# Transposes of attention and experts moved from TensorE to transposing DMAs, in a vision transformer block with routed experts

## The reference

```python
p = x.reshape(n, C, 14, 16, 14, 16).transpose(0, 2, 4, 1, 3, 5).reshape(n, 196, 768)
h = concat([class_token, einsum('npd,hd->nph', p, W) + b], 1) + pos_embed     # 64 x 197 x 192
# local attention: 12 heads of 16, each token sees the 13 tokens around it
q, k, v = split(layernorm(h) @ w_qkv)
h = h + (softmax(q . k_window / 4) . v_window) @ w_proj + b_proj
# experts: 8, the best 2 of each token, weights made to sum to 1
probs = softmax(layernorm(h) @ router_w.T)
top_w, top_i = top_k(probs, 2)
h = h + sum_e w_e * (gelu(layernorm(h) @ w1[e] + b1[e]) @ w2[e] + b2[e])      # 192 -> 768 -> 192
```

## Time and profile before

| | us |
|---|---|
| median of 3 runs | 1631.99 (1623.08 to 1639.81) |
| profiled execution | 1638.75 |
| its span, first to last instruction | 1637.0 |
| busy: TensorE, VectorE, GpSimd, ScalarE | 1471.8, 1114.5, 856.6, 721.7 |
| mean granted TensorE clock | 0.959 of full |

### The profile page before, as it was taken

One profiled execution on the slowest core, in us unless ns is written; L12 is line 12 of the kernel. 1 busy time (PEld: TensorE's weight loads), 2 busy tenths in 40 slices (PEclk: granted clock), 3 DMA queues, 4 the chain that ended last, 5 costly groups with the idle time before them and its releaser, 6 DMA issues. The chain is left out here.

```text
span 1637.0 us, 52314 instructions
## 1 busy us (share of the span) xinstructions
PE 1471.8 (90%) x18345; PEld 1222.1 (75%) x18346; DVE 1114.5 (68%) x2883; ACT 721.7 (44%) x1209; POOL 856.6 (52%) x900
## 2 busy tenths in 40 slices
PE   5999999998989999998643999999999999999995
PEld 4787888877878887887532777777777777777774
DVE  2577878777877787776554666666666666666663
ACT  2455554454545544454222444444444444444441
POOL 4235665555655665565441555555555555555554
PEclk9999999999999999999656999999999999999998
DMA  5665656556565657554314344444344444444432
GB/s 168 176 180 157 195 142 189 158 158 190 148 189 145 198 141 200 153 149 114 91 43 142 59 60 59 61 61 64 59 59 59 61 59 61 59 61 61 65 36 30
DMA packets 190165, 182.64 MB, mean 112 GB/s; under 512 B 86362, under 2 KB 166438, under 8 KB 188990
## 3 DMA queue, kind: packets, MB, share of 16 engines
q1 hardware_dynamic: 125834, 111.46, 25.1%
q0 software_dynamic: 41680, 41.84, 17.4%
q10 hardware_dynamic: 22499, 27.28, 5.3%
HBM read 104.93 MB, written 65.29 MB: 104 GB/s over the span
## 5 line engine op out<-in xcount | busy, mean ns | idle before, releaser
L992 POOL DMA_INDIRECT out<-y,token x219 | 368.6, 1683 | 73.6 <-issue 72.8
L1100 PE MATMUL down<-w_hi,g_hi 128*128 x1314 | 323.6, 246 | 2.1 <-DVE y L1066 1.1
L1102 PE MATMUL down<-w_hi,g_lo 128*128 x1314 | 323.0, 246 | 0.0
L1101 PE MATMUL down<-w_lo,g_hi 128*128 x1314 | 322.9, 246 | 0.0
L1088 PE MATMUL up<-e_xT,w_hi 128*128 128x384 f16 x1314 | 286.7, 327 | 0.0
L1013 ACT ACTIVATE act_out<-up,bias 128x384 f32<-128x384 f32 x438 | 251.2, 582 | 73.1 <-PE up L1088 73.0
L390 POOL DMA_INDIRECT sorted_scratch<-payload,place x212 | 220.1, 1038 | 59.7 <-issue 56.7
L779 PE MATMUL near<-we,patches 128*120 128x192 f32 x1272 | 223.9, 333 | 18.6 <-DMA patches<-in_xt 10.9
L1005 ACT COPY e_xT<-turned 128x1152 f16<-128x1152 f16 x73 | 81.7, 1119 | 353.0 <-PE turned L1080 353.0
L779 PEld LDWEIGHTS near<-we,patches 128*120 128x120 f32 x1272 | 208.1, 185 | 28.9 <-issue 28.1
L1049 DVE TENSOR_TENSOR g_lo<-act_out,g_hi 128x768 f16<-128x768 f32 x219 | 210.0, 959 | 7.6
(11 more groups left out here) (155 smaller groups left out, 2680.9 us busy)
## 6 DMA issues: line engine op xcount, KB each, us to landing
patches<-in_xt SPq DMA_DIRECT2D x53, 720.0 KB
rows<-sorted_scratch SPq DMA_DIRECT2D x73, 301.5 KB, 2.8
v_diag<-v_scratch SPq DMA_DIRECT2D x159, 89.2 KB
v_scratch<-v_rows SPq DMA_DIRECT2D x53, 191.2 KB, 3.3
tab<-tab_scratch SPq DMA_DIRECT2D x53, 180.0 KB
out<-h ACTq DMA_DIRECT2D x52, 180.0 KB
stage<-in_w ACTq DMA_DIRECT2D x8, 1152.0 KB
k_diag<-qk SPq DMA_DIRECT2D x424, 15.8 KB
```

The source lines that it names most:

```text
L992: pool.indirect_dma_start(out=out, out_offset=bass.IndirectOffsetOnAxis(ap=token[k][:, n:n + 1], axis=0), in_=y[k % 2][:, n, :], in_offset ...
L1100: pe.matmul(dst, g_hi[k % 2][:, m, cols], high, start=(m == 0), stop=False)
L1101: pe.matmul(dst, g_hi[k % 2][:, m, cols], low, start=False, stop=False)
L1102: ins = pe.matmul(dst, g_lo[k % 2][:, m, cols], high, start=False, stop=(m == MF - 1))
```

## The change

Seven sets of edits:

- `turn` and the identity are gone. SP issues a transposing DMA (`transpose=True`, SBUF to SBUF) for the normalised tokens, one for the attention output, and two for the routed tokens. `xs1` and `payload` get 128 partitions, and are cleared at the start; TensorE waits for the DMAs' semaphores `x1_in` and `x2_in`. ScalarE's copies 480 and 491 are gone; copy 485 now reads the transposed slots in SBUF, and waits for `oT_in`.
- TensorE's order: the probabilities' transposes stand ahead of counting.
- VectorE: `route_steps(grp, 2)` stands behind the normalisation, together with part 3.
- SP's order: transpose of the normalised tokens, 8 key copies, transpose of the output, transposes of the routed tokens, `v_diag`. The key copies and `v_diag` stand one iteration earlier in SP's stream.
- Value store, patches (now two blocks ahead), table and mask are issued by ScalarE, behind the high halves of the normalised tokens.
- The tables are built in `v_diag` and no longer in `payload`, so that `v_diag` is cleared after they are stored.
- Experts: each batch is loaded transposed straight from the sorted DRAM scratch into one of four `e_xT` buffers, and its 18 last columns (number, weights) by a second DMA. The transposes, `take` and the PSUM tensor `turned` are gone; four up banks in place of three.

```diff
@@ SP, attention_part
             def body(t):
-                g, a = t - 2, t - 4
-                if runs(t, 4):
+                g, a, d, b = t - 1, t - 3, t - 5, t - 6
+                if runs(t, 1):
+
+                    sp.wait_ge(s["lo1"], g + 1)
+                    need(sp, s["v_done"], g)
+                    sp.dma_start(xT1[:].rearrange("p n c r -> p (n c) r"), xs1[:].rearrange("p n c -> p (n c)"), transpose=True)\
+                      .then_inc(s["x1_in"], 16)
+                if runs(t, 3):
 
                     sp.wait_ge(s["qk_lo_set"], min(a + 2, BLOCKS))
                     need(sp, s["scored"], 2 * a)
                     for h in range(8):
                         sp.dma_start(*key_halves(h, a)).then_inc(s["k_diag_set"], 16)
+                if runs(t, 5):
+
+                    sp.wait_ge(s["o_lo_set"], d + 1)
+                    need(sp, s["oT_set"], d)
+                    sp.dma_start(oT_slots[:].rearrange("p n c r -> p (n c) r"), os_[:].rearrange("p n c -> p (n c)"), transpose=True)\
+                      .then_inc(s["oT_in"], 16)
+                if runs(t, 6):
+
+                    sp.wait_ge(s["lo2"], b + 1)
+                    need(sp, s["routed"], b)
+                    for n in range(2):
+                        sp.dma_start(xT2[:, n], payload[:, 2 * (b % RING) + n, 0:NUMBER_AT].bitcast(F16), transpose=True)\
+                          .then_inc(s["x2_in"], 16)
...
@@ ScalarE, attention_part
                 if runs(t, 5):
 
-                    act.wait_ge(s["o_turned"], d + 1)
+                    act.wait_ge(s["oT_in"], 16 * (d + 1))
                     need(act, s["proj_done"], d)
...
+                if runs(t, 1):
+
+                    act.wait_ge(s["v_set"], g + 1)
+                    act.dma_start(v_dram[REACH + SPAN * g:REACH + SPAN * g + SPAN, :].rearrange("(n p) c -> p n c", n=2),
+                                  v_rows[:].rearrange("p n h d -> p n (h d)")).then_inc(s["v_out"], 16)
+                if runs(t + 2, 0):
+                    act.wait_ge(s["embedded"], t + 1)
+                    act.dma_start(patches[t % 2][:], xt[t + 2]).then_inc(s_patch[t % 2], 16)
+                    if t == 0:
+                        act.wait_ge(s["tab_out"], 16)
+                    act.wait_ge(s["h1_set"], t + 1)
+                    load_tab(act, t + 2)
+                if runs(t, 3) and a + 1 < BLOCKS:
+                    need(act, s["scored"], 2 * a)
+                    load_band(act, a + 1)
...
@@ TensorE, attention_part
                 if runs(t, 1):
 
-                    pe.wait_ge(s["xT_set"], g + 1)
+                    pe.wait_ge(s["x1_in"], 16 * (g + 1))
                     need(pe, s["qk_main"], g)
...
                 if runs(t, 6):
 
-                    pe.wait_ge(s["xT2_set"], b + 1)
...
+                    pe.wait_ge(s["x2_in"], 32 * (b + 1))
+                    pe.wait_ge(s["h2_set"], min(d, BLOCKS))
...
@@ experts_part
-                sp.dma_start(rows[k][:], sorted_dram[bass.ds(row, BATCH), :].rearrange("(p r) c -> p r c", r=PARTS))\
+                sp.dma_start(xT[k][:], sorted_dram[bass.ds(row, BATCH), 0:NUMBER_AT].bitcast(F16), transpose=True).then_inc(s_xT[k], 16)
+                sp.dma_start(rows[k][:], sorted_dram[bass.ds(row, BATCH), NUMBER_AT:PAYLOAD].rearrange("(r p) c -> p r c", r=PARTS))\
                   .then_inc(s_rows[k], 16)
...
-                    need(sp, s["turned"], u - 1)
+                    need(sp, s["up_done"], MF * (u - 1))
                     need(sp, s["meta_set"], u - 1)
                     load(u + 2, (k + 2) % 4)
...
             def body(u, k, p):
-                if not last(u, 1):
-                    turn(u + 2, (k + 2) % 4, p + (k + 2) // 4)
                 if not last(u):
-                    up_product(u + 1, k + 1, expert_of(pe, u + 1))
+                    up_product(u + 1, (k + 1) % 4, p + (k + 1) // 4, expert_of(pe, u + 1))
                 down_product(u, k, expert_of(pe, u))
```

More of the change, by code:

```diff
@@ L440, in _ @@
                 act.mul(bp[row:row + 1, :], bp32[row:row + 1, :], WS).then_inc(s["weights"], 1)
-            def pieces(bank):
-                return bank[:].bitcast(F16)[:, 0:6 * ROWS].rearrange("p (n c r) -> p n c r", n=2, c=3)
             def body(t):
@@ L759, in _ @@
         def _(pe):
-            def turn(src, dst, place):
-                rows = src.shape[0]
-                for n in range(2):
-                    for c in range(3):
-                        at = place(n, c)
-                        ins = pe.transpose(dst[:, at:at + rows], src[:, n, 128 * c:128 * c + 128], ident16[0:rows, 0:rows])
-                return ins
             def body(t):
@@ L789, in body @@
                 grp, counted = groups(t, 8)
+                if runs(t, 4):
+                    pe.wait_ge(s["exp_set"], c + 1)
+                    for n in range(2):
+                        for m in range(QUADS):
+                            ins = pe.transpose(scores[0:VKEYS, n, 128 * m:128 * m + 128],
+                                               prob[:, n, TRIO * m:TRIO * m + TRIO, :].rearrange("p h c -> p (h c)"), identf[:])
+                        ins.then_inc(s["prob_turned"], 1)
                 if counted:
@@ L926, in sem @@
             return ctx.enter_context(nc.semaphore(name))
-        rows = [sb(f"rows{k}", [128, PARTS, PAYLOAD], U16) for k in range(4)]
+        rows = [sb(f"rows{k}", [128, PARTS, PAYLOAD - NUMBER_AT], U16) for k in range(4)]
         token = [sb(f"token{k}", [128, PARTS], U32) for k in range(4)]
@@ L933, in experts_part @@
         bias = [sb(f"bias{k}", [128, MF], F32) for k in range(2)]
-        xT = [sb(f"e_xT{k}", [128, PARTS, 3, 128], F16) for k in range(2)]
+        xT = [sb(f"e_xT{k}", [128, 3, BATCH], F16) for k in range(4)]
         act_out = sb("act_out", [128, MF, BATCH], F32)
@@ L1103, in down_product @@
                 ins.then_inc(s["down_done"], 1)
-            turn(0, 0, 0)
-            turn(1, 1, 0)
-            up_product(0, 0, expert_of(pe, 0))
+            up_product(0, 0, 0, expert_of(pe, 0))
             def body(u, k, p):
-                if not last(u, 1):
-                    turn(u + 2, (k + 2) % 4, p + (k + 2) // 4)
                 if not last(u):
-                    up_product(u + 1, k + 1, expert_of(pe, u + 1))
+                    up_product(u + 1, (k + 1) % 4, p + (k + 1) // 4, expert_of(pe, u + 1))
                 down_product(u, k, expert_of(pe, u))
```

179 lines of the change are left out of this document (62 added, 117 removed).

## The result

The changed kernel takes **1965.14 us** (median of 4 runs, 1960.00 to 1969.53) beside 1632.60 for the kernel before: 1.204 of it, 95% interval [1.197, 1.211]. Forecast was 1625 in a range of 1582 to 1692. Forecast was next to no change (0.4% faster); the direction, the size and the range were wrong.

The account below looks back on a forecast made before the run. Experts were taken as bound by TensorE, attention by waits on the path through the router. Terms -35.5 + 26 - 8 + 5 + 6 = -6.5 us gave 1632.3 against the profiled execution, 1625 against the median; range 1582 to 1692.

Parts of the forecast that it names:

- The expert stage: Expert loop on TensorE: nine turns removed per batch, 0.50 us each set, 71 sets, -35.5 us; transposing load hidden.
- I take 2.9 from issue to landing and 0.35 per issue.: Attention stage, SP: assumed times of each 96 KB transposing DMA, taken from near the plain value store.
- +1.0 us for each of 26 iterations.: Attention, low halves to router: 3.35 us instead of 2.36 in iterations that don't count; +26 us in all.
- pieces one after another: Rival, transposing DMAs: 128-column pieces go one by one, two DMAs 7.9 us; +340 us, beyond 1900; chance 0.05.
- SP's chain: Rival, SP's queue of keys, output, routed tokens: transposes hold SP 1.1 and 0.6 us; +50 us, 1682; chance 0.22.
- The transposes of normalised tokens fit.: Attention, SP: issued after v_diag at 574.83, landing near 578, before qk needs them at 579.9; no cost.
- Counting iterations, -8.: Attention, iterations that count: VectorE's wait for the qk copy shrinks, 0.3 us in each of 27; -8 us.
- ScalarE's four issues, +5.: Attention, ScalarE: value store, patches, table, mask take 1.8 us in 1.6 idle; 0.2 us in 24 iterations, +5 us.
- The DMA engines.: Rival, attention stage: 2304 small packets per block at 52 ns fill the DMA engines, 16.3 us a block; +49, 1681; chance 0.11.

Follow-up runs that it names:

- run 1: Attention stage of the kernel before with the changed kernel's experts stage; 1568.75 us, 0.9754 of the kernel before.
- run 3: Separate small program without the model, timing transposing DMAs and plain copies alone and beside other loads; 192 KB transpose: 1.21 us issue, 2.8 us to landing.
- run 6: Changed kernel with the normalised tokens' transpose issued ahead of the value windows in SyncE's queue; 1937.7 us, -26.
- run 13: Changed kernel with all four transposes of a block on ScalarE's queue and all twelve key copies on SyncE's; 1804.1 us, -160 against the changed kernel.
- run 4: Changed kernel without patch loads after the second block; 1900.4 us, -63 against the changed kernel's 1963.9.
- run 12: Attention of before, new experts, weight loads in six parts, and only the normalised tokens' turn replaced by a DMA last in SyncE's turn; 0.9836 of before.
- run 10: Changed kernel with each expert's weights loaded in six parts in six blocks; 1953.9 us.
- run 9: Changed kernel with SyncE's eight key copies moved behind the transposes of output and routed tokens, ahead of the value windows; 1953.6 us.
- run 5: Changed kernel without SyncE's eight key copies from the second block on; 1849.7 us, -114 against the changed kernel.

## Why the prediction was wrong

**The expert stage: right.** Forecast -35.5, measured -41 (run 1), and 38.6 us between the first and the last up products of the changed kernel. The batch lost 0.53 us (10.01 to 9.48) where 0.50 was forecast, and hiding the load held.

**"I take 2.9 from issue to landing and 0.35 per issue."** The first half held for a transfer without neighbours (2.3 to 2.9), not beside patches (5.5). The second was the first failed step: 1.18 to 1.25 us per transpose, whether 96 or 192 KB. I reasoned from the plain store because both are "one DMA of 128 partitions". The Trainium skill's page "Advanced Engine Details and Errata", X-Bar Transpose (TRN2), says that transposing DMAs are as fast as ordinary ones. Run 3 comes near that for the transfer, 2.8 us against 2.1 for a plain copy of 192 KB, a third longer, and not for the issue, 1.21 against 0.46. For "pieces one after another" I had estimated 7.9 us for two transposes from the Trainium skill's page "VectorE: DVE Perf Modes", The three transpose paths; measured were 2.5 of issue and 1.15 to landing.

**"+1.0 us for each of 26 iterations."** This is the step that failed most. I took the transposes as a delay in one path, from low halves to router, with SyncE free of its keys in time. With four transposes of 1.24 us and more, SyncE's turn is 15 us, and as the value windows wait for the attention-value products of the block before, the turn and the path add up to a loop of 22.6 us in which nothing overlaps. My rival "SP's chain" named the place and the order of keys, output, routed tokens, and two prices: 1.1 us for 192 KB was close, 0.6 for 96 KB half of it; but it charged +2.6 us on half of the blocks, since it too left out what stands ahead of the keys. Runs 6 and 13 bear this out: moving one item inside the queue trades waits (-26), taking the same transposes to the other queue gives 160 us back.

**"The transposes of normalised tokens fit."** They don't: TensorE's qk waits 97.0 us in 32 blocks for them, and their issue takes 2.6 us in the median. The windows ahead of it are not what stretches it (1.21 us behind windows in run 3); without the patches loads it is 1.36 (run 4), and issued ahead of the windows 1.21 (run 6). I had costed them at nothing and given as cover the time up to qk in the old schedule, which moved along.

**Counting iterations, -8.** No such gain is seen, as all blocks are on the loop: VectorE's wait for the qk copy, 13.7 us in 21 iterations before, is 116.7 in 18 blocks from 200 to 1000 us, and its routing waits another 115.6 us for ScalarE's logit copy, so it isn't what comes late. No run isolates this term.

**ScalarE's four issues, +5.** No run isolates them. The exponential's wait behind ScalarE's own issues is 99.8 us in 29 of 36 blocks (200 to 1000 us) against 68.0 in 22 of some 44, and it lies beside SyncE's longer turn.

**The DMA engines.** The rival had +49 for packets of 52 ns. The packets did become small (329722 under 512 bytes against 86362), but cost 27 ns each (0.270 x 16 x 1967.7 / 318498). The share of DMA time is 0.69, not 0.9. But that is 0.69 of a longer block: 15.2 us of DMA time a block, where the kernel before had 8.9 (0.60 of 14.76) and the rival reckoned 16.3. Its packets were right too: (329722 - 200825) / 53 is 2430 small packets a block more than in run 1, for 2304. So the load that the rival named came, and only isn't what ends last while SyncE's loop takes 22 us. Run 4 measures what relief brings: 63 us for 720 KB a block.

**TensorE's clock** stood in no sum. It is a second loss: the stage has 29% idle time and a granted clock of 0.79, some 3 us per block by the split above. The windows above have it low behind the waits, and over whole executions it is mostly higher where the waits are shorter (0.852 in the changed kernel's profile, 0.884 in run 13, 0.960 in run 12), but run 10 has 0.842 with 1953.9 us. No run changes the clock alone, so how much of the 369 us would have gone with the waits is not shown.

**What stays open.** Run 13 still is 235 us above run 1. One transpose accounts for 21.5 (run 12). How the rest divides between the output's and the routed tokens' landings, the lower clock, and the DMA engines' load wasn't taken apart further. The last is a rival that no run settles: run 13's 14.6 us of DMA time a block are about the 14.15 us that a whole block takes in run 1, so a better order alone may not get the time of before back. Nor does any run give the loop second buffers: the windows wait for the products because `v_diag` is single, and with two of them the same queue might do.

## What to carry to other kernels

Before replacing work of a compute engine by DMAs, write down the whole turn of the queue that will issue them, each at its measured issue time, with the wait that its first item has; if an item waits for the end of the block and the next block waits for the turn's last item, the sum of the turn adds to the path and hides nothing. A transposing DMA is cheap where its source is known two periods ahead and the queue is empty (the experts, -41 us), and dear where producer and reader are a few microseconds apart. Moving one item within the full queue here mostly changed the name of the wait (runs 6 and 9); the second queue gave back 160 us of 354, and leaving the work where it was gave all.

## What the runs showed of the hardware

- A transposing DMA holds SyncE 1.18 to 1.25 us for 96 and for 192 KB (run 3 and the changed kernel, medians of undisturbed issues), 1.32 for 295 KB from DRAM (the experts' `L947`, median); a plain store 0.35, a plain copy within SBUF 0.46. On ScalarE it is 1.30 to 1.32 (run 13, medians).
- Behind the start of a 1.77 MB load the same issue took up to 11.95 us (run 5): the issuing engine is held, not only the landing.
- Beside one 720 KB load a 192 KB transpose lands after 5.5 us instead of 2.8, while its issue stays at 1.21 (run 3).
- With transposes and a large load together the DMA engines were 96% busy at 129 GB/s (run 5, 475 to 515 us); without transposes, the stage of before moves 167 GB/s at 60%.
- The kernel before itself differs by 1.8% between sets of runs (1609.6 to 1637.9 us), and the changed kernel hardly follows (1963.9 and 1965.1, beside 1610.0 and 1632.6): ratios of 1.221 and 1.204 for one and the same pair.
